# Router logits taken from the un-normalised x1, and the router's steps split around the expert matmuls

## The reference

```python
x = _layernorm(x + attn(x), axis=-1)            # x1, normalised
router_logits = x @ Wg.T                        # Wg: [8, 2048]
routing_weights = sigmoid(router_logits)
scores = routing_weights + bias
_, top_k_index = top_k(scores, 2)
top_k_weights = take_along_axis(routing_weights, top_k_index, axis=1)
top_k_weights = top_k_weights / top_k_weights.sum(axis=-1, keepdims=True)
expert_w = einsum('tk,tke->te', top_k_weights, one_hot(top_k_index, 8))
h1 = einsum('th,efh->tef', x, W1)
h3 = einsum('th,efh->tef', x, W3)
g = silu(h1) * h3 * expert_w[:, :, None]
x = _layernorm(x + einsum('tef,ehf->th', g, W2), axis=-1)
```

## Time and profile before

| | |
|---|---|
| three runs, us | 5534.89, 5449.39, 4808.92 |
| median | 5449.39 |
| the profiled execution (the third) | 4808.92 |
| its span, core 6 | 4807.3 |
| its shortest span, core 5 | 4778.9 |
| PE busy | 4052.3 us |
| DVE busy | 1151.8 us |
| ACT, POOL busy | 350.0 and 319.5 us |

### The profile page before, as it was taken

One profiled execution on the slowest core, in us unless ns is written; L12 is line 12 of the kernel. 1 busy time (PEld: TensorE's weight loads), 2 busy tenths in 40 slices (PEclk: granted clock), 3 DMA queues, 4 the chain that ended last, 5 costly groups with the idle time before them and its releaser, 6 DMA issues.

```text
span 4807.3 us, 46540 instructions; the slowest of 8 cores (4778.9 to 4807.3 us)
## 1 busy us (share of the span) xinstructions
PE 4052.3 (84%) x17449; PEld 1714.7 (36%) x17449; DVE 1151.8 (24%) x2023; ACT 350.0 (7%) x621; POOL 319.5 (7%) x602
## 2 busy tenths in 40 slices
PE   5699747479999999999959983747999999999994
PEld 1243312134444444444414331213344444444441
DVE  0121151411211211201262106141221121121126
ACT  0002101000000000000010210000000000000001
POOL 2100000000000000000100000000000000000000
PEclk5699969689999999999979996877899999999997
DMA  9743325324654444344544332632355434444442
GB/s 161 129 75 60 54 61 142 88 48 68 118 95 71 70 75 73 66 77 70 82 114 76 62 57 47 148 88 48 57 98 108 74 66 77 72 68 77 71 70 75
DMA packets 136778, 389.00 MB, mean 81 GB/s; under 512 B 15728, under 2 KB 23920, under 8 KB 136560
## 3 DMA queue, kind: packets, MB, share of 16 engines
q0 software_dynamic: 85392, 302.06, 38.0%
q1 hardware_dynamic: 32736, 58.78, 4.0%
q10 hardware_dynamic: 18432, 25.17, 1.6%
HBM read 646.03 MB, written 41.94 MB: 143 GB/s over the span
## 4 chain that ended last, share of the span: by engine, by line
PE 79%; DVE 10%; DMA 4%; issue 4%; ACT 2%; DVEq 0%; POOL 0%; ACTq 0%; PEldq 0%; SPq 0%; POOLq 0%
PE ps L935 20%; PE ps L953 19%; PE ps L1031 18%; PE ps L693 5%; PE ps L620 5%; PE ps L482 5%; PE ps L553 4%; DMA wring<-xpre 2%; DVE gbufS L1011 2%; DVE ntmpS L654 1%; DVE ygS L662 1%; DVE rstdR L409 1%; DVE ot2S L1120 1%; DVE ntmpS L648 1%; ACT sqS L734 1%
## 5 line engine op out<-in xcount | busy, mean ns | idle before, releaser
L935 PE MATMUL ps<-xnS,wring 128*128 128x512 bf16 x4096 | 957.8, 394 | 0.0
L1031 PE MATMUL ps<-gbufS,wring 128*128 128x512 bf16 x4096 | 927.4, 389 | 32.3 <-DVE gbufS L1011 32.3
L953 PE MATMUL ps<-xnS,wring 128*128 128x512 bf16 x4096 | 915.4, 382 | 0.0
L1031 PEld LDWEIGHTS ps<-gbufS,wring 128*128 128x128 bf16 x4096 | 406.4, 100 | 557.5 <-issue 98.8
L935 PEld LDWEIGHTS ps<-xnS,wring 128*128 128x128 bf16 x4096 | 412.4, 101 | 531.2 <-issue 97.0
L953 PEld LDWEIGHTS ps<-xnS,wring 128*128 128x128 bf16 x4096 | 403.4, 98 | 491.1 <-issue 34.1
L974 DVE TENSOR_TENSOR gbufS<-ps,sh1S 128x512 bf16<-128x512 f32 x256 | 165.0, 686 | 1618.8 <-PE ps L953 1388.4
L693 PE MATMUL ps<-ygS,wring 128*128 128x512 bf16 x1024 | 279.5, 434 | 120.0 <-DVE ygS L662 120.0
L968 ACT ACTIVATE sh1S<-ps 128x512 bf16<-128x512 f32 x256 | 138.9, 594 | 2529.3 <-PE ps L935 2486.5
L482 PE MATMUL ps<-xnS,wring 128*128 128x512 bf16 x1024 | 231.7, 385 | 55.0 <-ACT vS L509 39.1
L1056 DVE SCALAR_TENSOR_TENSOR x2S<-ps,x2S 128x512 f32<-128x512 f32 x192 | 132.8, 692 | 527.4 <-PE ps L1031 527.4
(11 more groups left out here) (128 smaller groups left out, 1431.6 us busy)
## 6 DMA issues: line engine op xcount, KB each, us to landing
wring<-w1T POOLq DMA_DIRECT2D x128, 512.0 KB, 5.8
wring<-w3T POOLq DMA_DIRECT2D x128, 512.0 KB, 5.8
wring<-w2T POOLq DMA_DIRECT2D x128, 512.0 KB, 6.1
wring<-xpre POOLq DMA_DIRECT2D x48, 512.0 KB, 9.9
xf32S<-xfm SPq DMA_DIRECT2D x64, 256.0 KB, 7.4
wring<-wvT POOLq DMA_DIRECT2D x32, 512.0 KB, 5.5
wring<-wqT POOLq DMA_DIRECT2D x32, 512.0 KB, 5.4
wring<-wgT POOLq DMA_DIRECT2D x32, 512.0 KB, 5.3
```

What stands on the lines that cost most here:

```text
L935: g1 = pr.step("pe", lambda en, kt=kt, c=c, slot=slot1: en.matmul(out=psS[c][:, 0:CW], lhsT=wringS[slot][:, kt * P:(kt + 1) * P], rhs=x1nS ...
L953: g3 = pr.step("pe", lambda en, kt=kt, c=c, slot=slot3: en.matmul(out=psS[2 + c][:, 0:CW], lhsT=wringS[slot][:, kt * P:(kt + 1) * P], rhs= ...
L1031: grp = pr.step("pe", lambda en, k=k, c=c, slot=slot2: en.matmul(out=psS[4 + c][:, 0:CW], lhsT=wringS[slot][:, k * P:(k + 1) * P], rhs=gbu ...
```

## The change

The logits are linear in x1, so with W the router's weights and w their sums over the features, W(x1 - mu)·rstd is (W x1 - w mu)·rstd. The change uses this. In the setup, w is formed by 16 matmuls with a column of ones. In the Wo loop each x1 tile's bf16 copy cbS, which the statistics read, is also multiplied by the router's weights, into ps0 and ps1. Behind the barrier the 32 matmuls over xnS are gone, and three DVE operations per column half correct the logits ahead of the sigmoid. Further, the router's tile is split in two: `emit_router_front` (first transpose and DVE's chain) stays ahead of the w1 group, and `emit_router_back` (second transpose and copy) is called behind the w3 group and the products.

```diff
+    wsum_grp = None
+    for kt in range(KT):
+        dep = [t_wgf, t_ones_bf]
...
+        wsum_grp = pr.step("pe", lambda en, kt=kt: en.matmul(
+            out=psS[5][0:E, 0:1], lhsT=wgfS[:, kt * E:(kt + 1) * E],
+            rhs=onescol_bf[:], start=(kt == 0), stop=(kt == KT - 1)),
+            deps=dep, inc="pe" if kt == KT - 1 else None)
+    t_wsum = pr.tick("dve", lambda en: en.tensor_copy(
+        out=wsumC[:], in_=psS[5][0:E, 0:1]), deps=[wsum_grp])
...
+                    depl = [tc_, t_wgf]
+                    if mt == 0:
+                        depl += psB[c].begin_write()
+                    rl_grp[c] = pr.step("pe", lambda en, mt=mt, c=c, cbslot=cbslot: en.matmul(
+                        out=psS[c][0:E, 0:CW],
+                        lhsT=wgfS[:, mt * E:(mt + 1) * E],
+                        rhs=cbS[:, cbslot * CW:(cbslot + 1) * CW],
+                        start=(mt == 0), stop=(mt == NH - 1)),
+                        deps=depl, inc="pe")
+                    cbbuf.read(rl_grp[c])
...
-            rl_grp = [None] * NCW
-            for kt in range(KT):
-                for c in range(NCW):
-                    dep = [t_wgf, t_x1n[kt]]
...
-                    rl_grp[c] = pr.step("pe", lambda en, kt=kt, c=c: en.matmul(
-                        out=psS[c][0:E, 0:CW],
-                        lhsT=wgfS[:, kt * E:(kt + 1) * E],
-                        rhs=x1nS[:, kt * TH + c * CW:kt * TH + (c + 1) * CW],
...
             for c in range(NCW):
+                tl1 = pr.tick("dve", lambda en, c=c: en.tensor_scalar(
+                    out=r8a[:, c * CW:(c + 1) * CW],
+                    in0=muB[0:E, c * CW:(c + 1) * CW],
+                    scalar1=wsumC[:, 0:1], scalar2=None, op0=ALU.mult),
+                    deps=[t_wsum, muB_b.ready] + bt2)
+                tl2 = pr.tick("dve", lambda en, c=c: en.tensor_tensor(
+                    out=r8a[:, c * CW:(c + 1) * CW],
+                    in0=psS[c][0:E, 0:CW],
+                    in1=r8a[:, c * CW:(c + 1) * CW], op=ALU.subtract),
+                    deps=[tl1, rl_grp[c]])
+                tl3 = pr.tick("dve", lambda en, c=c: en.tensor_tensor(
+                    out=r8a[:, c * CW:(c + 1) * CW],
+                    in0=r8a[:, c * CW:(c + 1) * CW],
+                    in1=rstdB[0:E, c * CW:(c + 1) * CW], op=ALU.mult),
+                    deps=[tl2, rstdB_b.ready])
...
-            def emit_router_tt(tt):
+            def emit_router_front(tt):
...
+                rt_pend[tt] = te2
+
+            def emit_router_back(tt):
+                te2 = rt_pend[tt]
                 d7 = psB[7].begin_write()
...
                         if first_expert and ft < TT:
-                            emit_router_tt(ft)
+                            emit_router_front(ft)
...
+                        if first_expert and ft < TT:
+                            emit_router_back(ft)
```

More of the change, by code:

```diff
@@ L194, in build @@
     ewbS = A("ewbS", [P, TH], F32)
+    wsumC = A("wsumC", [E, 1], F32)
     xnS = A("xnS", [P, KT * TH], BF16)
@@ L314, in build @@
     t_fbB = bcast16(fbiasS, fbB, [t_fbias], E)
+    wsum_grp = None
+    for kt in range(KT):
+        dep = [t_wgf, t_ones_bf]
+        if kt == 0:
+            dep += psB[5].begin_write()
+        wsum_grp = pr.step("pe", lambda en, kt=kt: en.matmul(
+            out=psS[5][0:E, 0:1], lhsT=wgfS[:, kt * E:(kt + 1) * E],
+            rhs=onescol_bf[:], start=(kt == 0), stop=(kt == KT - 1)),
+            deps=dep, inc="pe" if kt == KT - 1 else None)
+    psB[5].wrote(wsum_grp)
+    t_wsum = pr.tick("dve", lambda en: en.tensor_copy(
+        out=wsumC[:], in_=psS[5][0:E, 0:1]), deps=[wsum_grp])
+    psB[5].read(t_wsum)
     t_preW = []
@@ L674, in emit_half @@
             st2_sq = [None] * NCW
+            rl_grp = [None] * NCW
             x1w_toks = {}
@@ L819, in emit_half @@
             x1nS = xnS
-            t_x1n = [x1n_tok[(kt, NCW - 1)] if (kt, NCW - 1) in x1n_tok
-                     else x1n_tok[(kt, 0)] for kt in range(KT)]
             t_x1n = [None] * KT
@@ L825, in emit_half @@
                 t_x1n[kt] = max(toks, key=lambda t: t[1])
-            rl_grp = [None] * NCW
-            for kt in range(KT):
-                for c in range(NCW):
-                    dep = [t_wgf, t_x1n[kt]]
-                    if kt == 0:
-                        dep += psB[c].begin_write()
-                    rl_grp[c] = pr.step("pe", lambda en, kt=kt, c=c: en.matmul(
-                        out=psS[c][0:E, 0:CW],
-                        lhsT=wgfS[:, kt * E:(kt + 1) * E],
-                        rhs=x1nS[:, kt * TH + c * CW:kt * TH + (c + 1) * CW],
-                        start=(kt == 0), stop=(kt == KT - 1)),
-                        deps=dep, inc="pe" if kt == KT - 1 else None)
             for c in range(NCW):
@@ L842, in emit_half @@
             for c in range(NCW):
+                tl1 = pr.tick("dve", lambda en, c=c: en.tensor_scalar(
[3 more added lines that the diff above has]
+                    deps=[t_wsum, muB_b.ready] + bt2)
+                muB_b.read(tl1)
+                tl2 = pr.tick("dve", lambda en, c=c: en.tensor_tensor(
[3 more added lines that the diff above has]
+                    deps=[tl1, rl_grp[c]])
+                psB[c].read(tl2)
+                tl3 = pr.tick("dve", lambda en, c=c: en.tensor_tensor(
[3 more added lines that the diff above has]
+                    deps=[tl2, rstdB_b.ready])
+                rstdB_b.read(tl3)
                 t = pr.tick("act", lambda en, c=c: en.activation(
-                    out=r8a[:, c * CW:(c + 1) * CW], in_=psS[c][0:E, 0:CW],
-                    func=AF.Sigmoid), deps=[rl_grp[c]])
-                psB[c].read(t)
+                    out=r8a[:, c * CW:(c + 1) * CW],
+                    in_=r8a[:, c * CW:(c + 1) * CW],
+                    func=AF.Sigmoid), deps=[tl3])
                 t_rl.append(t)
@@ L851, in emit_half @@
             ew_done = []
-            def emit_router_tt(tt):
+            rt_pend = {}
+            def emit_router_front(tt):
                 d6 = psB[6].begin_write()
@@ L865, in emit_router_tt @@
                     out=ewtS[:, 0:E], in0=sctS[:, 0:E], in1=fbB[:, 0:E],
-                    op=ALU.subtract), deps=[tev, t_fbB])
+                    op=ALU.subtract), deps=[tev, t_fbB] + ew_done[-1:])
                 tm8 = pr.tick("dve", lambda en: en.max(
@@ L983, in emit_half @@
                             pend[(ft, c)] = tg1
+                        if first_expert and ft < TT:
+                            emit_router_back(ft)
                     if first_expert:
                         for tt in range(FT, TT):
-                            emit_router_tt(tt)
+                            emit_router_front(tt)
+                            emit_router_back(tt)
                         first_expert = False
```

## The result

The ratio to the kernel before is 0.973, with an interval of 0.970 to 0.976; repeated (last experiment) it is 0.975, 0.973 to 0.977. The profiled execution took 4671.8 us, the one of before 4808.9.

The account below looks back on a forecast made before the run. PE, busy 84%, bounds the kernel, losing time to standstill and lower clock. 50.1 + 49.1 + 14.9 - 5 = 109 us off 4808.92 gives 4700, or 4678 without the disturbance; 4689 us was put between, range 4638 to 4732.

Parts of the forecast that it names:

- the anchor: Whole kernel: the 109 us gain was set against the profiled run's 4808.92 us, not the shown median of 5449.39.
- part 3: Wo loop: 64 added logit matmuls fit in PE's waits, taken as 0; bounds 27 us loss, 51 us gain.
- part 1: Expert 0: DVE's router chain hidden behind w1 and w3 groups, saving 50.1 us in half 0 and 49.1 in half 1.
- The second way of reckoning: Expert 0, cross-check: 72.0 us of waits plus 14 x 1.76 of clock, together 96.6 against 99.2.
- The end of expert 0: Before expert 1: DVE's products and the copy now come first, costing 1.7 us twice, perhaps 1.7 of clock: 5 us.
- Part 2: Start behind the barrier: logits moved ahead, first w1 load becomes the bound; gains 9.2 and 5.7, 14.9 us.
- DVE's path: Start behind the barrier: DVE's logit corrections let the first transpose run 6.1 us after POOL's first weight issue.
- Rival B: Wo turns: added matmuls keep the clock up, saving 1.69 us a group, 51 us more, 4638; chance 0.10.
- Part 4: Setup: 16 one-column matmuls and one copy, during waits for ACT and loads; taken as 0, bounds 0 and 1.5 us.
- The disturbance: Core 6, half 1's expert 0: slow clock, accounting for 22 us; 4678 if it doesn't return, 4700 otherwise.
- Rival D: Expert stage: denser PE work lowers the granted clock to 0.81, 1.45 us a group, 4967 for one half; chance 0.04.
- Rival C: Expert 0's router loop: the chain still holds PE before 14 groups, giving back 35 us, 4724; chance 0.08.

Follow-up runs that it names:

- experiment 1: Kernel before with only the router tile split in two, logits left behind the barrier; ratio 0.978 (0.976 to 0.981).
- experiment 3: Kernel before with 20 dummy matmuls between the two transposes of each router tile, the wait kept; ratio 0.995 (0.993 to 0.997).
- experiment 5: Changed kernel with the first four weight columns of expert 0 loaded ahead of the barrier; ratio 0.969 (0.953 to 0.985).
- experiment 2: Changed kernel without the split: logits in the Wo loop, second transpose ahead of its w1 group again; ratio 0.996 (0.994 to 0.998).
- experiment 4: Changed kernel with 15 of 16 logit matmuls per column half taken out of the Wo loop; profiled run 4676.9 us.
- experiment 6: Kernel before with 12 dummy matmuls in the waits of each Wo turn; two comparable runs 4755.4 and 4759.0 us.
- experiment 9: Changed kernel run once more with no edit, against the kernel before; ratio 0.975 (0.973 to 0.977), median of all runs 4674.1 us.

## Why the prediction was right or wrong

**The time and the anchor.** 4689 was given, and the changed kernel took 4671.8 in its profiled run; the range of 4638 to 4732 holds it. The gain was given as 109 us or 2.3%, and is 121 us on the cores' medians, 2.5 to 2.7% in the ratios. Two steps failed. The first is the one that relates the number to the runs of before: "The median of the three runs shown is 5449.39, 13% above the profiled run; the forecast is for runs like the profiled one". Set against the 5449.39 that stood in the figures, 4689 says 14% faster, five times what the change brings; even the medians over every run, 5034.1 and 4685.8, lie only 7% apart. The fourteen runs of before in this comparison go from 4794 to 5535 us, so three of them gave no base. A forecast in absolute time has to go with a base of the same kind, and only the 2.3% in the text did. The second is a term of the sum, the Wo loop, taken as 0 and measured at 7.5 us (part 3 below). That the number came out close rests on the large terms, which held; in part 1 two smaller errors cancelled, and that is luck.

**Part 1, the chain.** Forecast 50.1 and 49.1 us, measured 50.1 and 49.2 up to the first spread, and shown to be the split's by experiment 1. Two of its pieces were off and cancelled: the pairs of transposes cost 0.36 us (950.46 to 950.82), not 0.57, 1.5 less over the seven, and the measured 117.2 already holds the 1.8 us of wait at the end. The second way of reckoning, 14 x 1.76 us of clock = 24.6, took one group of the earlier trace rows for all. The eight groups of half 0 lose 2.54, 1.76, 1.19, 2.76, 1.87, 1.24, 2.79 and 1.88: 13.5 without the first, 27 for both halves, so this term was 2 us short. With the first it is 16.0, which is what experiment 3 gave back (16.1 and 15.4, against 24 expected). The end of expert 0, reckoned from the first spread and not from the last w3 matmul as its sentence says, was forecast at 5 us in all and costs 5.3: the wait of 1.8 in both halves, and the lower clock behind it mostly in half 1, since in half 0 most cores had it before.

**Part 2, the start.** The mechanism held in full: the w1 load became the bound, as experiment 5 shows, at 8.2 and 8.3 us of gain, 16.5 together against 14.9. DVE's path, reckoned at 6.1 us from POOL's issue to the transpose, took 5.1 (923.88 to 928.99). The Trainium skill's fit for such a load ("DMA: Bandwidth & Descriptors", anatomy of one DMA), an estimate of 3.2 us for 512 KB, would have put DVE's path last; after the change the load takes 9.7 us, and the trace disagrees again.

**Part 3, the Wo loop.** Taken as 0; it brings 5 to 9 us (the change 7.5, experiment 2 8.6, experiment 4 5.1). This is the term that was mis-sized. "Four leave the clock falling" was read from one turn; of the 15 groups behind a turn on core 0, half 0, four took 7.08 us even before. The change doesn't stop the fall, it makes it rarer and shorter: five of 15, and the others 8.0 to 8.6 instead of 8.3 to 8.8. Rival B was thus partly true, but its bound of 30 x 1.69 = 51 was too high for the same reason: experiment 6, with no slow group left, brings 36. Why two more matmuls make the fall rarer no run shows.

**Part 4** cost nothing measurable: the setup's 16 matmuls lie at 12.74 to 13.28 us, in PE's wait for preWb, and the first Wo matmul of half 0 starts at 599 to 603 us on all cores, as before.

**The disturbance.** I had put half of core 6's 22 us into the number (core 7 had it too: both took 179 to 180 us for expert 0 of half 1, the others 166). It didn't return in the profiled run, which is most of the distance from 4689 to 4671.8 (11 of 17 us). It was not the change's doing: the profiles of experiment 3, with the old order of the work, and of experiment 9, with the new, show no such core either. Rival D's price didn't come due in the profiled run: the dense stretch of the earlier trace rows stayed at a granted clock of 1.00, on core 1 as on the seven others:

```profile
1110.00:1150.00 40.00, 40.00 (x187) 18.16 (x186) 3.86 (x6) 3.26 (x6) 3.17 (x6) 1.00 0.45 74
```

Rival C, a wait left in the loop, is refuted by the rows of L886 and L943, which have no idle time before them from the second tile on.

## What to carry to other kernels

A chain on another engine that interrupts PE costs twice, by its length and by the clock behind it: here 34 and 13 us a half. The cure is to start the chain ahead of a block of matmuls and fetch its result behind it. When reckoning the clock's part, read all the groups behind such waits and not one, and look up what is issued at the barrier: once a wait is removed there, the next one is often a load that could have been issued earlier.

## What the runs showed of the hardware that I had not expected

The clock's part of a short wait isn't a constant. Behind waits of nearly one length the w1 groups took from 8.27 to 9.87 us, and the two longest waits (5.40 us, the others 5.04) had the two shortest groups behind them, 8.27 and 8.32. Behind Wo turns of 4.3 to 4.9 us some groups took 7.08 and most 8.3 to 8.8 (core 0, half 0). Useless matmuls in these waits made every group 7.07 or 7.08 us (experiments 3 and 6), and the kernel before 24 to 33 us faster with the same waits. The filling itself can run at the lower level: in experiment 3, the 20 dummies of the first tile come behind 3.2 us of idle time on every core, and took 4.49 us at a granted clock of 1.00 on core 3 in half 0, but 7.21 at 0.61 there in half 1, longer than the chain that they were to cover. Twelve of the sixteen took about 7 us, and the start grew by 2 to 3 us.
